# Loading the q and k rows of a graph attention layer: twelve loads of each block from GpSimd, or the late ones from SyncE inside the first pass

## The chip, the cores and the metric

One core of one Trainium2 chip runs the whole program as one launch. The metric is the device time of that core in microseconds, and lower is better. It is given as the median of three runs.

## The reference, cut to what matters

Four graph layers follow each other on 3125 nodes with 64 features and 100,000 edges. The last one is the attention layer, and the change lies around its inputs:

```python
h = jnp.maximum(_layernorm(x, axis=-1), 0.0)
q = (h[rows] @ qTrans).reshape(-1, 4, 16)
k = (h[cols] @ kTrans).reshape(-1, 4, 16)
v = (h[cols] @ vTrans).reshape(-1, 4, 16)
att = jnp.exp(jnp.clip(jnp.einsum('ehd,ehd->eh', q, k), -10.0, 10.0))
att = att / (segment_sum(att, rows)[rows] + 1e-08)
x = x + segment_sum((att[:, :, None] * v).reshape(-1, 64), rows)
```

## The kernel before, in words

The program is a sequence of three blocks, and every block ends in a barrier of all engines. `build_matrices` (line 122) scatters the edges into a dense table of edge counts and one of weights in DRAM. `propagating_layers` (line 687) runs the first three graph layers as six multiplications with these tables, and makes q, k and v for the fourth. `attention_layer` (line 1103) computes scores between all pairs of nodes and multiplies each with the edge count of the pair.

The nodes stand in 25 tiles of 128, and these in seven chunks (`CHUNKS`, line 44), six of 512 nodes and a last one of 128. At the end of `propagating_layers` TensorE projects chunk n to q and k (line 1032), and VectorE (`split`, line 895) cuts the result into three bf16 pieces; the last of the three is line 905. To reuse its piece buffer, `split(n)` waits until chunk n - 2 has been stored (line 900). GpSimd stores the pieces of chunk n in DRAM (line 1093, semaphore `rows_stored[n]`), waits until they have landed, and then issues twelve small loads (lines 1096 to 1100): six bring the k pieces and six the q pieces into the tile `held`, 16 partitions each, in the order in which the score matmuls want them. Such a load is called a placement below. A placement moves 64 KB for a chunk of 512 nodes and 16 KB for the last chunk. Then GpSimd turns to chunk n + 1:

```python
pool.wait_ge(rows_stored[n], 16)
for side, part_of in ((1, KPART), (0, QPART)):
    for i in range(NPART):
        pool.dma_start(placed[side][i * HD:(i + 1) * HD, :, cols], ...).then_inc(rows_placed[n], 16)
```

`attention_layer` goes over the q nodes in chunks (`ci`, seven passes), and in each pass over the 25 k tiles (`t`, called a step). In step t TensorE makes the scores of four heads (line 1317) from the k rows of tile t and the q rows of chunk ci, turns the edge counts of the step by four transposes (line 1324) and adds up the values of the step two before (line 1332). ScalarE takes the exponentials (lines 1192 to 1197), VectorE clips and weighs (lines 1224 to 1232), and GpSimd copies a value tile (line 1294).

SyncE loads the edge counts of each step (line 1168) into a ring of five buffers. The load of step t waits until the transposes of step t - 5 are done (line 1167). SyncE issues its loads in the order in which the program has them. In the first pass only, TensorE waits for `rows_placed[n]` ahead of the first k tile of chunk n (line 1351). Chunk 0 is waited for at the start of the block (line 1304). Passes 1 to 6 need the q rows of chunks 1 to 6, for which the same semaphores stand.

Of the kernel before, what the change touches and what calls it, by code (L numbers as in the profile page):

```python
# [16 lines left out]
P = 128  # L17
# [4 lines left out]
HD = D // HEADS  # L22
T = -(-N // P)
# [19 lines left out]
BANK = 512  # L43
CHUNKS = [(c, min(BANK, NR - c)) for c in range(0, NR, BANK)]
# [9 lines left out]
RING = 5  # L54
VW = 32
NPART = 6
QPART = [0, 0, 0, 1, 1, 2]
KPART = [0, 1, 2, 0, 1, 0]

# [9 lines left out]
def by_chunk(dram, n):  # L69

    c0, w = CHUNKS[n]
    return dram[c0 * NR:(c0 + w) * NR].rearrange("(p s c) -> p s c", p=P, s=T)


def rows_of(k):

    half = T * BANK // 2
    return [k["held"][0:NPART * HD, w * half:(w + 1) * half].bitcast(BF16).rearrange("p (h n) -> p h n", h=HEADS)
            for w in range(2)]


def gnn_layers(nc, x, src, dst, edge_weight, W_self, b_self, W_neigh, b_neigh,
               Wxz, bxz, bhz, Wxh, bxh, bhh, qTrans, kTrans, vTrans, out):
    with ExitStack() as ctx:
        def sb(name, shape, dt, c=ctx):
            return c.enter_context(nc.sbuf_tensor(name, shape, dt))

        table = nc.dram_tensor("table", [CELLS + GE, 2], F32, kind="Internal").ap()
        keys_dram = nc.dram_tensor("keys_dram", [NG, GE], F32, kind="Internal").ap()
        weights_dram = nc.dram_tensor("weights_dram", [NR * NR], F32, kind="Internal").ap()  # L90
        counts_dram = nc.dram_tensor("counts_dram", [NR * NR], F32, kind="Internal").ap()


        k = {
            "x": sb("x_nodes", [P, T, D], F32),
            "h": sb("h", [P, T, D], F32),
            "stat": sb("stat", [P, 3, T], F32),
            "acc": sb("acc", [P, T, D], F32),
            "held": sb("held", [P, T * BANK], F32),
            "ident": sb("ident", [P, P], F32),  # L100
            "deg_in": sb("deg_in", [P, T], F32),
            "deg_out": sb("deg_out", [P, T], F32),
            "w_self": sb("w_self", [D + 1, D], F32),
            "w_neigh": sb("w_neigh", [P, D], F32),
            "cheb0": sb("cheb0", [D + 1, 2 * D], F32),
            "cheb1": sb("cheb1", [P, 2 * D], F32),
            "cheb2": sb("cheb2", [P, 2 * D], F32),
            "qk": sb("qk", [D, 2 * D], F32),
            "v": sb("v", [D, D], F32),
        }  # L110
        parts_dram = nc.dram_tensor("parts_dram", [3, 2, HEADS, HD, NR], BF16, kind="Internal").ap()
        rows_placed = [ctx.enter_context(nc.semaphore(f"rows_placed{n}")) for n in range(len(CHUNKS))]
        with ExitStack() as c:
            build_matrices(nc, c, k, sb, table, keys_dram, weights_dram, counts_dram, x, src, dst, edge_weight,
                           W_self, b_self, W_neigh, b_neigh, Wxz, bxz, bhz, Wxh, bxh, bhh, qTrans, kTrans, vTrans)
        with ExitStack() as c:
            propagating_layers(nc, c, k, sb, weights_dram, counts_dram, parts_dram, rows_placed)
        with ExitStack() as c:
            attention_layer(nc, c, k, sb, counts_dram, rows_placed, out)


def build_matrices(nc, c, k, sb, table, keys_dram, weights_dram, counts_dram, x, src, dst, edge_weight,
# [564 lines left out]
                                        ALU.max, ALU.mult))  # L687


def propagating_layers(nc, c, k, sb, weights_dram, counts_dram, parts_dram, rows_placed):  # L690

    def sem(name):
        return c.enter_context(nc.semaphore(name))

    x, h, stat = k["x"], k["h"], k["stat"]
# [9 lines left out]
    resident = [k["held"][:].rearrange("p (s c) -> p s c", c=BANK), sb("resident", [P, T, BANK], F32, c)[:]]  # L705
    rest = term[:].rearrange("p t f -> p (t f)")
    parts = xs[:, 0].rearrange("p t f -> p (t f)")[:, 0:3 * BANK].bitcast(BF16).rearrange("p (b n c) -> p b n c", b=2, n=3)
    placed = rows_of(k)
    last = sb("last_chunk", [P, T, P], F32, c)
    clipped, scale = sb("deg_clipped", [P, 2, T], F32, c), sb("scale", [P, 7, T], F32, c)  # L710
    DINV, DIS, NDIS, INV, ROOT, TWICE, CHEB = range(7)
# [19 lines left out]
    h_ready, h_turned, h_copied = sem("h_ready_c"), sem("h_turned_c"), sem("h_copied_c")  # L731
    projected, values_made, values_copied = sem("projected"), sem("values_made"), sem("values_copied")
    parts_step, parts_ready = sem("parts_step"), sem("parts_ready")
    rows_stored = [sem(f"rows_stored{n}") for n in range(len(CHUNKS))]

    def tiles_of(n):
        c0, w = CHUNKS[n]
# [13 lines left out]
    with nc.Block() as block:  # L751
# [335 lines left out]
        @block.gpsimd  # L1087
        def _(pool):
            pool.wait_ge(sums_ready, NC * CHEB2 + KEPT[0] + 1)
            for n, (c0, w) in enumerate(CHUNKS):  # L1090
                cols = slice(c0, c0 + w)
                pool.wait_ge(parts_ready, n + 1)
                pool.dma_start(parts_dram[:, :, :, :, cols].rearrange("i w h d n -> (w h d) i n"), parts[:, n % 2, :, 0:w]  # L1093
                               ).then_inc(rows_stored[n], 16)
                pool.wait_ge(rows_stored[n], 16)
                for side, part_of in ((1, KPART), (0, QPART)):
                    for i in range(NPART):
                        pool.dma_start(placed[side][i * HD:(i + 1) * HD, :, cols],
                                       parts_dram[part_of[i], side, :, :, cols].rearrange("h d n -> d h n")
                                       ).then_inc(rows_placed[n], 16)  # L1100


def attention_layer(nc, c, k, sb, counts_dram, rows_placed, out):

    def sem(name):
        return c.enter_context(nc.semaphore(name))
# [5 lines left out]
    count = sb("count", [P, RING, 4, P], F32, c)  # L1112
# [11 lines left out]
    count_landed = [sem(f"count_landed{j}") for j in range(RING)]  # L1124
    counts_turned, weighted, values_added = sem("counts_turned"), sem("weighted"), sem("values_added")
# [9 lines left out]
    SC = T // 4  # L1135
# [15 lines left out]
    def over_chunks(eng, chunk):  # L1151

        with eng.Fori(0, SC) as ci:
            chunk(ci, 4)
        chunk(SC, T - 4 * SC)
# [4 lines left out]
    with nc.Block() as block:  # L1160
        @block.sync
        def _(sp):

            def chunk(ci, width):
                for t in range(T):
                    rows = by_chunk(counts_dram, t // 4)[:, bass.ds(4 * ci, width), t % 4 * P:(t % 4 + 1) * P]
                    sp.wait_ge(counts_turned, ci * T + t + 1)
                    sp.dma_start(count[:, t % RING, 0:width], rows).then_inc(count_landed[t % RING], 16)

            over_chunks(sp, chunk)  # L1170
            for f, ts in enumerate(out_parts):
                sp.wait_ge(out_ready, f + 1)
                full = slice(ts.start, min(ts.stop, T - 1))
                sp.dma_start(out[full.start * P:full.stop * P].rearrange("(t p) f -> p t f", p=P), tmp[:, full]
                             ).then_inc(out_stored, 16)
            sp.dma_start(out[(T - 1) * P:N], tmp[0:LAST, T - 1]).then_inc(out_stored, 16)
            sp.wait_ge(out_stored, 48)
# [123 lines left out]
        @block.tensor  # L1301
        def _(pe):
            pe.wait_ge(consts_set, 2)
            pe.wait_ge(rows_placed[0], 16 * 2 * NPART)
            pe.sem_inc(counts_turned, RING)
            pe.sem_inc(values_added, RING)

            def steps(ci, width, first=False):
# [27 lines left out]
                def step(t, j, n):  # L1336

                    score(t, j, ci * USES + n, ci * T + t)
                    add_values((j - 2) % RING, ci * T + t - 2)
# [4 lines left out]
                def tiles():  # L1344
                    pe.wait_ge(acc_read, ci + 1)
                    nc.tensor.matmul(acc[:, 0:W], zero_row[:, 0:P], zero_row[:, 0:W], start=True, stop=False,  # L1346
                                     skip_group_check=True)
                    if first:
                        for t in range(2, T):
                            if t * P % BANK == 0:  # L1350
                                pe.wait_ge(rows_placed[t * P // BANK], 16 * 2 * NPART)
                            step(t, t % RING, t // RING)
                        return
                    with pe.Fori(0, LOOPED // RING) as i:
                        for s in range(RING):
                            step(RING * i + 2 + s, (2 + s) % RING, i + (2 + s) // RING)
                    for t in range(2 + LOOPED, T):
                        step(t, t % RING, t // RING)
# [6 lines left out]
            def chunk(ci, width, next_width, first=False):  # L1365

                scores_of, tiles, values_of = steps(ci, width, first)
                tiles()
                for n in range(2):
                    if next_width:  # L1370
                        steps(ci + 1, next_width)[0](n)
                    values_of(T - 2 + n)
                pe.wait_ge(values_added, ci * T + T + RING)
                pe.sem_inc(acc_full, 1)
# [4 lines left out]
            with pe.Fori(1, SC - 1) as ci:  # L1379
                chunk(ci, 4, 4)  # L1380
# [32 lines left out]
```

## Time and profile before

| What | Value |
|---|---|
| median of three runs | 2637.91 us (2637.0 to 2641.92) |
| the profiled execution's own time | 2636.98 us |
| its span, first to last instruction | 2635.3 us |
| busy share of PE / DVE / ACT / POOL | 45% / 70% / 30% / 50% |
| mean granted TensorE clock | 0.982 |
| DMA, mean over the span | 204 GB/s |

PE is TensorE, PEld its weight loads, DVE is VectorE, ACT is ScalarE, POOL is GpSimd and SP is SyncE. A q behind an engine's name means its sequencer, which carries waits, drains, branches and the issue of DMAs. Line numbers are those of the kernel before. All stages come one after the other: the scatter of the edges until 1563 us, the six multiplications until about 2102 us, and the seven attention passes from 2135 us to the end.

### The profile page before, as it was taken

To read this page: it belongs to the slowest core of one execution; us is meant where nothing else is said; L and a number is where in the kernel's file an instruction comes from. 1 tells how busy PE (TensorE), PEld (TensorE's weight loads), DVE (VectorE), ACT (ScalarE), POOL (GpSimd) and SP (SyncE) were. 2 spreads that over 40 slices of the span, in tenths; PEclk is the share of its full clock that TensorE was granted. 3 is DMA by queue.
4 is the path that set the end of the run, shared out by engine and by line. 5 is a ranking of instruction groups with operands and counts; after the bars stand their busy time and mean duration, and the time that the engine had idled before them with its cause. 6 is when DMAs were issued, how large, how long until landed. Compare 5 with 4: busy or idle time off the path is not lost. (4 is left out here: it accounts for less than half of the span.)

```text
span 2635.3 us, 40047 instructions
## 1 busy us (share of the span) xinstructions
PE 1193.1 (45%) x12261; PEld 590.7 (22%) x12261; DVE 1857.5 (70%) x3958; ACT 795.0 (30%) x1929; POOL 1312.5 (50%) x1064
## 2 busy tenths in 40 slices
PE   2111111111111111111111019999999859889888
PEld 1111111111111111111111003344444412333334
DVE  9988788888888888888888510013222559999996
ACT  0000000122332233311111130000001359999996
POOL 2788888888888888888888800000000520000001
PEclk9999999999999999999999999999999879999997
DMA  7767677588988898866667599989987733333331
GB/s 231 240 192 228 195 226 202 124 211 208 225 195 223 204 223 202 218 140 130 140 137 167 116 303 424 385 342 386 424 365 277 221 94 86 86 88 88 87 88 45
DMA packets 489315, 537.88 MB, mean 204 GB/s; under 512 B 131264, under 2 KB 445117, under 8 KB 471069
## 3 DMA queue, kind: packets, MB, share of 16 engines
q1 hardware_dynamic: 123325, 283.04, 29.0%
q10 hardware_dynamic: 249904, 245.78, 28.9%
q0 software_dynamic: 116016, 8.23, 11.3%
q8 instruction: 31, 0.51, 0.1%
q14 instruction: 39, 0.32, 0.0%
HBM read 368.64 MB, written 168.31 MB: 204 GB/s over the span
## 5 line engine op out<-in xcount | busy, mean ns | idle before, releaser
L632 POOL DMA_INDIRECT table<-amount,cell x782 | 1220.1, 1560 | 294.3 <-issue 282.3
L453 DVE SCALAR_TENSOR_TENSOR equal<-key_row,keys,masks 128x1280 bf16<-128x1280 f32 (+9 forms) x790 | 692.0, 941 | 0.2 <-DVE parts L439 0.2
L585 PE MATMUL totals<-parts_g,equal 128*128 128x6 bf16 x4345 | 129.1, 167 | 1020.2 <-DVE is_tile L462 1020.0
L303 ACT ACTIVATE held<-held 128x128 f32<-128x128 f32 x600 | 179.2, 301 | 787.2 <-issue 776.4
L585 PEld LDWEIGHTS totals<-parts_g,equal 128*128 128x128 bf16 x4345 | 122.3, 104 | 1031.8 <-DVE is_tile L462 1031.4
L1063 PE MATMUL banks<-ring,xs 128*64 128x512 f32 x1200 | 290.5, 600 | 93.0 <-DMA ring<-counts_dram 91.7
L1093 POOL DMA_DIRECT2D parts_dram<-xs x7 | 5.5, 783 | 521.7 <-DVE xs L905 521.7
L1294 POOL COPY v_tile<-acc 128x64 f32 x175 | 41.5, 238 | 441.1 <-PE banks_d L1332 440.5
L445 DVE SCALAR_TENSOR_TENSOR equal_tail<-key_row,keys,masks 128x1280 bf16<-128x1280 f32 x156 | 235.2, 1545 | 18.2 <-issue 16.2
L1317 PE MATMUL banks_d<-held 96*128 (+2 forms) x700 | 192.9, 366 | 65.7 <-ACT att L1195 32.4
L1197 ACT ACTIVATE att<-att,shift 128x1024 f32<-128x1024 f32 (+1 forms) x175 | 209.5, 1197 | 0.0
L1192 ACT ACTIVATE att<-banks_d,shift 128x1024 f32<-128x1024 f32 (+1 forms) x175 | 201.5, 1151 | 19.7 <-PE banks_d L1317 19.3
L1229 DVE SCALAR_TENSOR_TENSOR att<-att,banks_d 128x1024 f32<-128x1024 f32 (+1 forms) x175 | 190.3, 1088 | 8.2 <-ACT att L1197 3.1
L1232 DVE TENSOR_TENSOR att<-att,banks_d 128x1024 f32<-128x1024 f32 (+1 forms) x175 | 188.9, 1080 | 0.0
L1195 ACT ACTIVATE att<-banks_d 128x1024 f32<-128x1024 f32 (+1 forms) x175 | 186.4, 1065 | 0.0
L1332 PE MATMUL banks_d<-att,v_tile 128*32 128x512 f32 (+1 forms) x1400 | 171.5, 565 | 0.5 <-DVE att L1232 0.5
L470 DVE TENSOR_REDUCE amount<-totals 128x20 f32<-128x60 f32 x79 | 17.4, 220 | 210.3 <-POOLq L646 160.7
L1063 PEld LDWEIGHTS banks<-ring,xs 128*64 128x64 f32 x1200 | 92.9, 137 | 261.9 <-issue 147.7
L303 ACT ACT_TABLE_LOAD x1 | 1.3, 1283 | 491.1 <-POOLq L646 491.1
L594 PE MATMUL totals<-carried_parts,equal_tail 128*128 128x6 bf16 x1560 | 54.4, 168 | 206.8 <-DVE carried_parts L490 204.3
L836 ACT COPY y_t<-banks 128x512 f32<-128x512 f32 (+1 forms) x42 | 22.7, 540 | 340.6 <-PE banks L1063 340.6
L925 DVE TENSOR_TENSOR xs<-banks,scale 128x256 f32<-128x256 f32 (+1 forms) x14 | 5.5, 396 | 164.1 <-PE banks L1009 164.1
(225 smaller groups left out, 1811.9 us busy)
## 6 DMA issues: line engine op xcount, KB each, us to landing
table<-acc ACTq DMA_DIRECT2D x100, 800.0 KB
held<-table ACTq DMA_DIRECT2D x24, 3200.0 KB
ring<-counts_dram SPq DMA_DIRECT2D x60, 1280.0 KB, 11.7
ring<-weights_dram SPq DMA_DIRECT2D x60, 1280.0 KB, 10.5
key_row<-keys_dram SPq DMA_DIRECT2D x79, 640.0 KB
weights_dram<-held ACTq DMA_DIRECT2D x24, 1600.0 KB
counts_dram<-c_tile ACTq DMA_DIRECT2D x24, 1600.0 KB
count<-counts_dram SPq DMA_DIRECT2D x150, 256.0 KB, 2.9
```

The lines of the kernel that those rows point to most:

```text
L303: ins = nc.scalar.activation(w_tile[:, b, s], cells[:, s, :, 0], ACT.Copy, accum_out=deg_parts[:, s, bass.ds(t, 1)])
L445: ins = nc.vector.scalar_tensor_tensor(equal_tail[:, b, i, :], key_row[:, b, :], keys[:, bass.ds(g * G - TAIL + i, 1)], all_mask, ALU.is_e ...
L453: ins = nc.vector.scalar_tensor_tensor(equal[b][:, OWN_AT[j]:OWN_AT[j + 1]], key_row[:, b, j * P:GE], keys[:, bass.ds(g * G + j, 1)], own_ ...
L585: nc.tensor.matmul(sums, equal[b][:, at:at + P], parts_g[:, b, j, :], start=False, stop=True, skip_group_check=True)
L632: nc.gpsimd.indirect_dma_start(out=table, out_offset=bass.IndirectOffsetOnAxis(ap=cell[:, b, j:j + 1], axis=0), in_=amount[:, b, j, :], in ...
L1063: ins = nc.tensor.matmul(banks[at:at + D, g % 2, 0:w], xs[:, prop % 2, s], rows, start=s < 2, stop=True, skip_group_check=True)
L1192: nc.scalar.activation(att[:, j, high, 0:W], scores[:, high, 0:W], ACT.Relu, bias=shift[:, 0:1]).then_inc(scores_read[1], 1)
L1195: nc.scalar.activation(att[:, j, low, 0:W], scores[:, low, 0:W], ACT.Exp).then_inc(scores_read[0], 1)
L1197: nc.scalar.activation(att[:, j, high, 0:W], att[:, j, high, 0:W], ACT.Exp, bias=shift[:, 1:2]).then_inc(expd_high, 1)
L1229: nc.vector.scalar_tensor_tensor(att[:, j, high, 0:W], att[:, j, high, 0:W], HI, times, ALU.min, ALU.mult)
L1232: nc.vector.tensor_tensor(att[:, j, low, 0:W], att[:, j, low, 0:W], times, ALU.mult).then_inc(weighted, 1)
L1317: ins = nc.tensor.matmul(scores[:, hd, 0:W], k6[:, hd, bass.ds(t * P, P)], q6[:, hd, bass.ds(ci * BANK, W)], start=True, stop=True)
```

## The change

GpSimd keeps storing all seven chunks. It places k for chunks 0 to 4 and q for chunk 0 alone. SyncE places k of chunks 5 and 6 behind its count loads 4 and 5 of the first pass (after waiting for the store of that chunk), and q of chunks 1 to 6 behind count loads 7 to 12. The semaphore `rows_placed` is split into `k_placed` and `q_placed`, and TensorE waits for `q_placed[1:]` at the end of the first pass. SyncE's first pass is written out, and its loop starts at pass 1.

```diff
+AHEAD = 5
+def place_rows(eng, k, parts_dram, side, n, placed):
+    cols = slice(CHUNKS[n][0], sum(CHUNKS[n]))
+    for i, part in enumerate((QPART, KPART)[side]):
+        eng.dma_start(rows_of(k)[side][i * HD:(i + 1) * HD, :, cols],
+                      parts_dram[part, side, :, :, cols].rearrange("h d n -> d h n")).then_inc(placed[n], 16)
...
                 pool.dma_start(parts_dram[:, :, :, :, cols].rearrange("i w h d n -> (w h d) i n"), parts[:, n % 2, :, 0:w]
                                ).then_inc(rows_stored[n], 16)
-                pool.wait_ge(rows_stored[n], 16)
-                for side, part_of in ((1, KPART), (0, QPART)):
-                    for i in range(NPART):
-                        pool.dma_start(placed[side][i * HD:(i + 1) * HD, :, cols],
-                                       parts_dram[part_of[i], side, :, :, cols].rearrange("h d n -> d h n")
-                                       ).then_inc(rows_placed[n], 16)
+                if n < AHEAD:
+                    pool.wait_ge(rows_stored[n], 16)
+                    place_rows(pool, k, parts_dram, 1, n, k_placed)
+                    if n == 0:
+                        place_rows(pool, k, parts_dram, 0, n, q_placed)
...
-            def chunk(ci, width):
+            def load(ci, width, t):
+                rows = by_chunk(counts_dram, t // 4)[:, bass.ds(4 * ci, width), t % 4 * P:(t % 4 + 1) * P]
+                sp.wait_ge(counts_turned, ci * T + t + 1)
+                sp.dma_start(count[:, t % RING, 0:width], rows).then_inc(count_landed[t % RING], 16)
+            for t in range(T):
+                load(0, 4, t)
+                n = t - RING + 1
+                if AHEAD <= n + AHEAD < len(CHUNKS):
+                    sp.wait_ge(rows_stored[n + AHEAD], 16)
+                    place_rows(sp, k, parts_dram, 1, n + AHEAD, k_placed)
+                n = t - RING - 1
+                if 1 <= n < len(CHUNKS):
+                    place_rows(sp, k, parts_dram, 0, n, q_placed)
+            with sp.Fori(1, SC) as ci:
                 for t in range(T):
...
-            over_chunks(sp, chunk)
+                    load(ci, 4, t)
+            for t in range(T):
+                load(SC, T - 4 * SC, t)
...
-            pe.wait_ge(rows_placed[0], 16 * 2 * NPART)
+            pe.wait_ge(k_placed[0], 16 * NPART)
+            pe.wait_ge(q_placed[0], 16 * NPART)
...
-                                pe.wait_ge(rows_placed[t * P // BANK], 16 * 2 * NPART)
+                                pe.wait_ge(k_placed[t * P // BANK], 16 * NPART)
...
                 tiles()
+                if first:
+                    for placed in q_placed[1:]:
+                        pe.wait_ge(placed, 16 * NPART)
```

## Rows read from the trace of the kernel before

**Rows 1.** The page, the span in 40 equal slices, TensorE.
```profile
PE   2111111111111111111111019999999859889888
```

**Rows 2.** Waits that ended between 2110 and 2240 us: total, times, longest.
```profile
PE banks_d L1317 <- ACTq L1184: 32.3, 1, 32.3
```

**Rows 3.** Line 751, the block's end: duration ns min/median/max, first and last start us.
```profile
L751 DVEq DRAIN  x1: 17/17/17, 2106.0 to 2106.0; - x1
L751 POOLq DRAIN  x1: 8400/8400/8400, 2125.9 to 2125.9; - x1
...
L751 SPq EVENT_SEMAPHORE  x1: 17/17/17, 2134.5 to 2134.5; - x1
```

**Rows 4.** Timeline of GpSimd: start us, us, instruction, and the idle time before it.
```profile
2074.40 6.09 POOL L1098 DMA_DIRECT2D held<-parts_dram  x12 [17.20 <-DMA parts_dram<-xs]
2080.48 0.77 POOL L1093 DMA_DIRECT2D parts_dram<-xs  x1
2083.73 6.09 POOL L1098 DMA_DIRECT2D held<-parts_dram  x12 [2.48 <-DMA parts_dram<-xs]
...
2118.21 0.77 POOL L1093 DMA_DIRECT2D parts_dram<-xs  x1
2120.72 6.09 POOL L1098 DMA_DIRECT2D held<-parts_dram  x12 [1.74 <-DMA parts_dram<-xs]
```

**Rows 5.** DMA issues from 2030 to 2240 us: KB each, median us to landing.
```profile
held<-parts_dram POOLq DMA_DIRECT2D x72, 64.0 KB, 2.4
parts_dram<-xs POOLq DMA_DIRECT2D x6, 384.0 KB, 3.0
held<-parts_dram POOLq DMA_DIRECT2D x12, 16.0 KB, 2.0
```

**Rows 6.** Timeline of VectorE, the last piece of chunks 3 to 6.
```profile
2083.35 0.43 DVE L905 CAST xs<-term 128x512 bf16<-128x512 f32 x1
...
2096.96 0.43 DVE L905 CAST xs<-term 128x512 bf16<-128x512 f32 x1
...
2103.81 0.43 DVE L905 CAST xs<-term 128x512 bf16<-128x512 f32 x1
...
2105.51 0.23 DVE L905 CAST xs<-term 128x128 bf16<-128x128 f32 x1
```

**Rows 7.** Windows: each engine's busy us, granted clock, DMA share, GB/s.
```profile
2040.00:2060.00 20.00, 20.00 (x106) 8.63 (x104) 8.88 (x20) 6.34 (x11) 7.98 (x14) 1.00 1.02 364
2116.00:2117.00 1.00, 0.00 (x0) 0.00 (x0) 0.00 (x0) 0.00 (x0) 1.00 (x3) 0.50 0.52 135
2128.00:2129.00 1.00, 0.00 (x0) 0.00 (x0) 0.00 (x0) 0.00 (x0) 0.00 (x0) 0.50 0.00 0
```

**Rows 8.** Line 208, the end of the block before: GpSimd's drain.
```profile
L208 POOLq DRAIN  x1: 1052/1052/1052, 1528.5 to 1528.5; - x1
```

**Rows 9.** Line 1168, the count loads until 2240 us: issue, landing, timeline.
```profile
L1168 SPq DMA_DIRECT2D count<-counts_dram x39: 346/373/400, 2135.3 to 2238.3; - x39
DMA to landing us min/median/max: 2.7/2.9/5.5
2135.26 103.42 SPq L1168 DMA_DIRECT2D count<-counts_dram  x39
```

**Rows 10.** Timeline of TensorE, the transposes of steps 0 and 13.
```profile
2138.43 1.11 PE L1324 MATMUL banks_d<-ident,count 128*128 128x128 f32 x4 [1.29 <-DMA count<-counts_dram]
...
2176.95 0.63 PE L1324 MATMUL banks_d<-ident,count 128*128 128x128 f32 x4
```

**Rows 11.** Line 248, SyncE's small loads at the start of the program.
```profile
L248 SPq DMA_DIRECT2D cheb<-in_L_gnn_Wxz_dram x5: 596/597/607, 36.5 to 39.7; - x5
...
L248 SPq DMA_DIRECT2D x_nodes<-in_x_dram x2: 1269/5684/10100, 20.7 to 22.1; - x2
...
L248 SPq DMA_DIRECT2D self_in<-in_L_gnn_W_self_dram x1: 940/940/940, 32.2 to 32.2; - x1
```

More of the change, by code:

```diff
@@ L111, in gnn_layers @@
         parts_dram = nc.dram_tensor("parts_dram", [3, 2, HEADS, HD, NR], BF16, kind="Internal").ap()
-        rows_placed = [ctx.enter_context(nc.semaphore(f"rows_placed{n}")) for n in range(len(CHUNKS))]
+        rows_stored, q_placed, k_placed = [[ctx.enter_context(nc.semaphore(f"{name}{n}")) for n in range(len(CHUNKS))]
+                                           for name in ("rows_stored", "q_placed", "k_placed")]
         with ExitStack() as c:
@@ L116, in gnn_layers @@
         with ExitStack() as c:
-            propagating_layers(nc, c, k, sb, weights_dram, counts_dram, parts_dram, rows_placed)
+            propagating_layers(nc, c, k, sb, weights_dram, counts_dram, parts_dram, rows_stored,
+                               q_placed, k_placed)
         with ExitStack() as c:
-            attention_layer(nc, c, k, sb, counts_dram, rows_placed, out)
+            attention_layer(nc, c, k, sb, counts_dram, parts_dram, rows_stored, q_placed, k_placed, out)
 def build_matrices(nc, c, k, sb, table, keys_dram, weights_dram, counts_dram, x, src, dst, edge_weight,
@@ L687, in layer_norm, with propagating_layers @@
                                         ALU.max, ALU.mult))
-def propagating_layers(nc, c, k, sb, weights_dram, counts_dram, parts_dram, rows_placed):
+def propagating_layers(nc, c, k, sb, weights_dram, counts_dram, parts_dram, rows_stored, q_placed, k_placed):
     def sem(name):
@@ L707, in propagating_layers @@
     parts = xs[:, 0].rearrange("p t f -> p (t f)")[:, 0:3 * BANK].bitcast(BF16).rearrange("p (b n c) -> p b n c", b=2, n=3)
-    placed = rows_of(k)
     last = sb("last_chunk", [P, T, P], F32, c)
@@ L733, in propagating_layers @@
     parts_step, parts_ready = sem("parts_step"), sem("parts_ready")
-    rows_stored = [sem(f"rows_stored{n}") for n in range(len(CHUNKS))]
     def tiles_of(n):
@@ L1094, in _, with attention_layer @@
                                ).then_inc(rows_stored[n], 16)
-                pool.wait_ge(rows_stored[n], 16)
-                for side, part_of in ((1, KPART), (0, QPART)):
-                    for i in range(NPART):
-                        pool.dma_start(placed[side][i * HD:(i + 1) * HD, :, cols],
-                                       parts_dram[part_of[i], side, :, :, cols].rearrange("h d n -> d h n")
-                                       ).then_inc(rows_placed[n], 16)
-def attention_layer(nc, c, k, sb, counts_dram, rows_placed, out):
+                if n < AHEAD:
[3 more added lines that the diff above has]
+                        place_rows(pool, k, parts_dram, 0, n, q_placed)
+def attention_layer(nc, c, k, sb, counts_dram, parts_dram, rows_stored, q_placed, k_placed, out):
     def sem(name):
@@ L1162, in _ @@
         def _(sp):
-            def chunk(ci, width):
+            def load(ci, width, t):
[12 more added lines that the diff above has]
+            with sp.Fori(1, SC) as ci:
                 for t in range(T):
-                    rows = by_chunk(counts_dram, t // 4)[:, bass.ds(4 * ci, width), t % 4 * P:(t % 4 + 1) * P]
-                    sp.wait_ge(counts_turned, ci * T + t + 1)
-                    sp.dma_start(count[:, t % RING, 0:width], rows).then_inc(count_landed[t % RING], 16)
-            over_chunks(sp, chunk)
+                    load(ci, 4, t)
+            for t in range(T):
+                load(SC, T - 4 * SC, t)
             for f, ts in enumerate(out_parts):
```

## The prediction, made before the changed kernel was run

> **What bounds the kernel now.** I read the page's slices first. TensorE is busy nearly throughout from slice 24 on, except for a dip around slice 32 [rows 1]. That is where the six multiplications end and the attention begins. The waits of that stretch name the dip: the first score matmul waited 32.3 us [rows 2]. The record at the block's end tells who came last. VectorE had its drain done at 2106.0. GpSimd's drain started at 2125.9 and took 8.40 us, to 2134.3, and all engines were released at 2134.5 [rows 3]. So the 28 us from 2106 to 2134 belong to GpSimd alone. Its timeline shows what it did: for each chunk a store, a wait of about 2.5 us until the store had landed, and a burst of twelve placements of 6.09 us. The last burst ran from 2120.72 to 2126.81 [rows 4]. The pieces it waited for came much earlier: the last was cast at 2105.51 + 0.23 = 2105.74 [rows 6]. GpSimd is behind by its own issuing. Behind its last issue lie another 7.5 us of drain (2126.81 to 2134.3), although the last placements take 2.0 us to land [rows 5] and nothing moved from 2128 on [rows 7].
>
> A burst costs the same 6.09 us for 64 KB and for 16 KB placements [rows 4, 5], 0.51 us each, so the issue and not the data sets it.
>
> **The change part by part.**
>
> GpSimd's chain. It loses 48 of 84 placements: 24 us of issuing at 0.51. It also loses two waits, those for stores 5 and 6. The sum cannot be 24 plus two waits, for GpSimd would then run into VectorE's pieces. I follow the chain. Chunk 0 and store 1 do not change, so GpSimd goes on at 2074.40 with six placements instead of twelve: 3.05 us, to 2077.45. A store costs 3.25 us until the burst behind it starts (2080.48 to 2083.73) [rows 4]. Chunk 2 is thus done at 2077.45 + 3.25 + 3.05 = 2083.75. Chunk 3's pieces are ready at 2083.35 + 0.43 = 2083.78 [rows 6], so it is done at 2090.1. Chunk 4's pieces are ready at 2097.39, and it is done at 2103.7. From here VectorE is the later one: chunk 5's pieces are ready at 2104.24, its store is issued by 2105.0, chunk 6's pieces are ready at 2105.74, and the last store is issued by 2105.74 + 0.77 = 2106.5. Nothing waits behind it. VectorE itself is not helped or hurt: for chunk 6 it needs store 4 landed, which comes at 2097.4 + 3.25 = 2100.7. GpSimd's last issue ends at 2106.5 instead of 2126.8, **20.3 us earlier**.
>
> The drain behind it. Of a drain behind two stores no row exists, so I bound it. Now it is 7.5 us behind the last issue [rows 3, 4]. The other end is the drain of the block before, 1.05 us [rows 8], where every DMA had landed when it began. If the drain is that short once the stores have landed (3.0 us from issue [rows 5]), it ends at 2105.74 + 3.0 + 1.05 = 2109.8; the lowest end, 1.05 us behind the last issue, is 2107.6. I take 7.5 us, as the nearest row: the same block, direct DMAs, and 6 us of it with no data moving. GpSimd's drain then ends at 2106.5 + 7.5 = 2114.0, against 2134.3. With the short drain the gain is 24.5 to 26.7 us.
>
> The loads on SyncE. It issues 48 placements, 12 for k of chunks 5 and 6 behind count loads 4 and 5, and 36 for q behind loads 7 to 12. Its waits for `rows_stored` 5 and 6 hold up count load 5 and all behind it, but the stores land by about 2109, before SyncE leaves the barrier. What matters is the count ring. SyncE starts at 2135.26 in the old time frame [rows 9]. Load 13 is the first behind all placements. It is used by the transposes of step 13, which start at 2176.95 [rows 10]. Ahead of its landing lie 14 count loads of 0.37 us plus a move, 0.41 each, so 5.7 us, then 48 placements of c us, and 2.9 us of landing [rows 9]. That fits if 48c is at most 2176.95 - 2135.26 - 5.7 - 2.9 = 33.1 us, **c at most 0.69 us**. SyncE never issued such a placement. The nearest by form is the count load, 0.37 us. The small loads of the start, by far nearer in their 64 short rows, cost 0.60 us, one of them 0.94 [rows 11]. I take 0.60 as the value, between these: no stall, with 4 us to spare. At 0.94 the stall is 48 x 0.25 = 12 us. Data does not fill the queue: the six 64 KB placements of one step are 384 KB, 2.9 us at the 135 GB/s that GpSimd's bursts reached [rows 7], and all of them together some 19 us, in 42 us.
>
> The waits on TensorE. The k rows of chunk 5 are wanted at step 20 and the q rows at the end of the pass, both behind step 13. So they cost nothing. If the cover were gone, a late q would delay pass 1 by as much as it is late.
>
> The first steps. After the gap the four transposes of step 0 took 1.11 us, those of step 13 0.63 [rows 10], since the granted clock was 0.50, the lower of its two levels (1.2 GHz), throughout the gap [rows 7]. A gap shorter by 20 us still lies in that stretch, so the start-up of the pass is moved and not changed: nothing.
>
> **Sum.** 20.3 us less, nothing given back. The profiled execution took 2636.98 us around its span of 2635.3; it would take 2616.7. The median of the runs is 0.9 us above the profiled one, so I forecast 2617.6.
>
> **The rivals.**
>
> Short drain. The 7.5 us may hang on the number of DMAs still queued (two against twelve), or only on their landing. For it speaks the 1.05 us of [rows 8], against it that in [rows 7] nothing moved in the last 6 us. Time: 2637.9 - 24.5 to 26.7 = 2611.2 to 2613.4.
>
> SyncE's issuing shows, mildly. If c is 0.7 to 1.1, TensorE waits for counts between steps 8 and 13, the stall is 0 to 20 us, at 0.94 12 us: 2629.6. For it speaks the 0.94 row, against it the 0.37 of the count loads.
>
> Slower than before. The same queue, from a definite point on: the gain of 20.3 is used up at c = 0.69 + 20.3/48 = 1.11 us, and 0.2% is lost at 1.22. Only the two loads of the nodes [rows 11], of 1.27 us and 10.1 us, were dearer; they stood behind large loads in a full queue. At 1.27 us the stall is 28 us and the time 2645.4. The place would be the transposes of line 1324 in steps 8 to 13.
>
> Nothing gained. The transfers themselves may be the bound, so that GpSimd would be held by them wherever they are issued. Against it: 16 KB and 64 KB cost the same issue, and the DMAs ran at 135 GB/s there where the same queues gave 364 in the multiplications [rows 7]. Time: 2637.9. The Trainium skill (DMA: Bandwidth & Descriptors, "Issuing engines are not separate DMA queues") speaks for this rival: all engines' DMAs run on the same 16 DMA engines, and issuing from several only saves the sequencer's issue time, which it calls usually small. By that rule the change would give little. Here the trace disagrees in the size: issuing is 0.51 us for each placement, 24 us for the 48.
>
> **How the numbers follow.** Forecast 0.52, with its own range of 2615 to 2620 (the drain and chain uncertain by 1 to 2 us); short drain, or one between the two ends, 0.28; SyncE's stall 0.13; slower 0.03; nothing gained 0.04. The range runs from 2610.5, just below the shortest drain, to 2624, which takes in stalls up to 6 us, c = 0.82. It leaves out the dearer half of the stalls and the last two cases, plus what I have not thought of. A measurement tells apart about 0.2%, 5.3 us. Faster by more than that: 0.52 + 0.28 + 0.12, so 0.92. Within it 0.05, slower 0.03.
>
> **What would show it.** In the changed trace GpSimd's last store should be issued at about 2105.7, and its drain should end at about 2114. A drain of 1 to 4 us is the short one. The wait of the first score matmul should fall from 32.3 to about 12 us. SyncE's placements should take 0.3 to 0.7 us each. TensorE's wait for counts should stay at the first step, and the first pass should last as long as now. The forecast is wrong if the drain differs by over 3 us, if TensorE waits for counts in steps 5 to 13, or if the first pass grows by over 3 us.

## The result, and the profile after

The changed kernel took 2613.82 us (median of five runs, 2613.0 to 2618.17), against 2639.74 us for the kernel before in the same comparison (2637.0 to 2641.92). The ratio is 0.9906, with a 95% interval of 0.9893 to 0.9920. The profiled execution took 2614.88 us around a span of 2613.2, which is 22.1 us less span. The medians are 25.9 us apart, and no trace accounts for the 3.8 us between the two figures: the kernel before was slower here than in its own profile (2639.74 against 2636.98 us), and the changed one faster (2613.82 against 2614.88 us).

The page's slices show the dip of [rows 1] filled. It is 7 and 9 now, where 8 and 5 stood:

```profile
PE   1111111111111111111111109999999979889888
```

The waits that ended between 2090 and 2240 us. The first line answers to [rows 2]; the second is the only wait of the transposes' matmuls for counts:

```profile
PE banks_d L1339 <- ACTq L1205: 8.5, 1, 8.5
...
PE banks_d L1346 <- DMA count<-counts_dram: 1.1, 1, 1.1
```

The block's end, now line 760 (answers to [rows 3]). VectorE is done at 2106.8, GpSimd's drain ends at 2106.8 + 4.36 = 2111.2, and all are released at 2111.3. From VectorE's end to the release it was 28.5 us and is 4.5:

```profile
L760 DVEq DRAIN  x1: 17/17/17, 2106.8 to 2106.8; - x1
L760 POOLq DRAIN  x1: 4360/4360/4360, 2106.8 to 2106.8; - x1
L760 SPq EVENT_SEMAPHORE  x1: 17/17/17, 2111.3 to 2111.3; - x1
```

The timeline of GpSimd (answers to [rows 4]). From chunk 1 on a burst has six placements and takes 3.06 to 3.42 us, and the last two stores have no burst behind them:

```profile
2074.98 3.06 POOL L87 DMA_DIRECT2D held<-parts_dram  x6 [16.64 <-DMA parts_dram<-xs]
2078.03 0.77 POOL L1102 DMA_DIRECT2D parts_dram<-xs  x1
2081.34 3.18 POOL L87 DMA_DIRECT2D held<-parts_dram  x6 [2.53 <-DMA parts_dram<-xs]
...
2105.16 0.77 POOL L1102 DMA_DIRECT2D parts_dram<-xs  x1 [0.19 <-issue]
2106.84 0.76 POOL L1102 DMA_DIRECT2D parts_dram<-xs  x1 [0.91 <-DVE xs L914]
```

The timeline of SyncE's queue in the first pass, and behind it line 87 on that queue. Bursts of six placements and count loads alternate, and load 13 leaves at 2143.06. A placement takes 0.43 us, about 0.48 with the gap behind it (2.85 / 6 = 0.475):

```profile
2111.95 2.90 SPq L1176 DMA_DIRECT2D count<-counts_dram  x5
2114.90 3.04 SPq L87 DMA_DIRECT2D held<-parts_dram  x6
...
2140.16 2.85 SPq L87 DMA_DIRECT2D held<-parts_dram  x6
2143.06 96.33 SPq L1176 DMA_DIRECT2D count<-counts_dram  x34
```
```profile
L87 SPq DMA_DIRECT2D held<-parts_dram x48: 303/426/508, 2114.9 to 2142.6; - x48
```

The first pass grew by 0.2 us at most: from the release to VectorE's copy of its result it takes 83.7 us (2111.3 to 2195.01), before 83.5 (2134.5 to 2218.04). The copy, before and after:

```profile
2218.04 0.68 DVE L1241 COPY o_t<-banks_d 128x512 f32 x1
```
```profile
2195.01 0.68 DVE L1262 COPY o_t<-banks_d 128x512 f32 x1
```

The release came 23.2 us earlier (2134.5 to 2111.3), although the block's own end slipped by 0.8 us with VectorE (2106.0 to 2106.8). Of these 23.2 us, 1.1 were given back by the end of pass 5, which the section on the hardware takes up.

### The profile page after: what moved, and what is told of

Read it like the earlier page. It is cut to its first block and busy times, and to the rows that moved or that the text cites. A ratio compares the mean times of both kernels' runs of the same rounds, so it can differ in the third digit from the quotient of the medians.

```text
span 2613.2 us, 39974 instructions
## 1 busy us (share of the span) xinstructions
PE 1194.5 (46%) x12261; PEld 590.1 (23%) x12261; DVE 1858.3 (71%) x3958; ACT 794.9 (30%) x1929; POOL 1288.5 (49%) x1016
```

## The experiments

Two things were open: what sets GpSimd's drain, and how near the count ring came to a stall. A drain is the instruction with which an engine's queue ends the block. In what follows "the tail" is the time from the end of GpSimd's last issue to the end of its drain: 7.5 us before, 3.6 us after (2107.60 to 2111.2).

### Does waiting for the landing shorten the drain?

```diff
+            for n in range(AHEAD, NC):
+                pool.wait_ge(rows_stored[n], 16)
```

> The changed kernel, but GpSimd waits at the end of the block until stores 5 and 6 have landed, and only then drains. Nothing else differs. Theory A (the drain clears up after every DMA that GpSimd issued in the block, 43 here, 91 before, so it takes longer the more there were): the wait changes nothing, since that clearing up goes on whether or not the landing is waited for; the drain still ends about 2.2 us behind the landing, 3.6 us behind the last issue. Theory B (the drain waits for DMAs that are still under way, with some microseconds of extra for those): with none under way it takes the 1.05 us of the block before, and ends 1.1 us behind the landing, 1 us earlier than now. Theory C (a fixed time behind the last issue): as A.

Line 760 and GpSimd's next instruction:

```profile
L760 POOLq DRAIN  x1: 3567/3567/3567, 2109.4 to 2109.4; - x1
```
```profile
2106.89 0.75 POOL L1102 DMA_DIRECT2D parts_dram<-xs  x1 [0.90 <-DVE xs L914]
2113.21 0.63 POOL L1307 MEMSET v_tile<- 128x640 f32 x1 [5.56 <-POOLq L760]
```

With everything landed the drain starts at 2109.4 and still takes 3.57 us. It ends at 2113.0, 1.8 us later than without the wait, and 5.3 us behind the last issue. Theory B falls, and so does theory C. Theory A as written (the clearing goes on beside the wait) falls too: the time is spent in the drain itself, and only once it has started. What the drain does in it no trace shows.

The same for the kernel before:

```diff
+            pool.wait_ge(rows_placed[NC - 1], 16 * 2 * NPART)
```

> The kernel before, but GpSimd waits for the landing of its last twelve placements ahead of its drain. Landing comes about 2 us behind the last issue, and the drain ended 7.5 us behind the last issue. Theory A (clearing up, counted by the DMAs of the block): the drain still ends about 7.5 us behind the last issue, 5.5 us or so behind the landing. Theory B (only DMAs under way cost): the drain takes 1.05 us behind the landing and the gap of TensorE shrinks by 4.5 us, from 32.3 to 28.

```profile
L751 POOLq DRAIN  x1: 7487/7487/7487, 2129.0 to 2129.0; - x1
```

The drain takes 7.49 us with nothing under way. It took 3.57 with 43 DMAs in the block and 7.49 with 91: 3.92 us for 48 DMAs, 0.082 us each, and 43 x 0.082 = 3.5 leaves nothing fixed. Both kernels were released about 2 us later with their wait (2113.1 instead of 2111.3, and 2136.6 instead of 2134.5). The one run of each took 2617.28 and 2639.97 us.

The price is GpSimd's. SyncE had issued 142 loads in this block (120 into `ring`, 22 into other tiles), and its own drain took 0.12 us, before and after:

```profile
L751 SPq DRAIN  x1: 123/123/123, 2056.3 to 2056.3; - x1
```
```profile
L760 SPq DRAIN  x1: 124/124/124, 2056.9 to 2056.9; - x1
```

### The count of DMAs: fewer, more, tiny, early

`AHEAD = 3`, so 31 DMAs on GpSimd:

> AHEAD = 3 instead of 5: GpSimd places k of chunks 0 to 2 and q of chunk 0 (24 placements and 7 stores, 31 DMAs, against 43), SyncE places k of chunks 3 to 6 in the first pass. The last two stores are the same. Theory A (0.08 us of drain for each DMA of the block, from 91 against 43): the drain ends 3.6 - 12 x 0.08 = 2.6 us behind the last issue, and the gap shrinks by 1 us. Theory B (those under way) and C (fixed part behind two stores): 3.6 us as now. SyncE has 60 placements of 0.475 us in its first pass: 28.5 us, under the budget of 33, so no wait for counts at steps 5 to 16; k of chunk 3 is wanted at step 12 and issued by step 3.

The tail is 2.8 us (2105.61 to 2108.4), as theory A has it within 0.2. SyncE issued 60 placements in the first pass. TensorE's matmuls waited for counts only at the first step, as before; its weight loads waited three more times, 0.4 to 0.6 us each between 2144 and 2151, and the pass took 82.9 us, no longer than now. The one run took 2613.29 us.

Forty-eight more DMAs, ahead of everything:

```diff
+            for i in range(48):
+                pool.dma_start(spare[0:1, i:i + 1], weights_dram[i:i + 1].rearrange("(a b) -> a b", a=1)
+                               ).then_inc(spare_landed, 16)
+            pool.wait_ge(spare_landed, 16 * 48)
             pool.wait_ge(sums_ready, NC * CHEB2 + KEPT[0] + 1)
```

> The changed kernel, in which GpSimd issues 48 more loads of a single number each at the start of the block, some 450 us ahead of its first store, and waits for all of them. 91 DMAs in the block as before the change, but 48 of them one row and long done. Theory A in its plain form (each DMA of the block costs the drain 0.082 us): the drain ends 7.5 us behind the last issue instead of 3.6, and the release moves from 2111.3 to 2115.2. Theory A' (what counts is rows, or DMAs of the last burst): 3.6 as now, or little more.

Line 761, the block's end of this kernel, and the last store:

```profile
L761 POOLq DRAIN  x1: 8273/8273/8273, 2101.2 to 2101.2; - x1
```
```profile
2101.19 0.75 POOL L1107 DMA_DIRECT2D parts_dram<-xs  x1 [0.91 <-DVE xs L915]
2109.69 0.63 POOL L1310 MEMSET v_tile<- 128x640 f32 x1 [7.76 <-POOLq L761]
```

The tail is 7.5 us (2101.94 to 2109.5): that of the kernel before, with the DMAs of the kernel after and 48 single numbers that had landed some 450 us earlier. (Its build of the matrices ended 6 us earlier, so the time of its one run, 2612.16 us, says nothing here.)

The same with 64 rows each:

```diff
+            for g in range(8):
+                for i in range(NPART):
+                    pool.dma_start(spare[i * HD:(i + 1) * HD], weights_dram[0:HD * HEADS * P // 2].rearrange(
+                        "(h d n) -> d h n", h=HEADS, d=HD)).then_inc(spare_landed, 16)
+                pool.wait_ge(spare_landed, 16 * NPART * (g + 1))
```

> As the kernel with 48 more one-number loads, but each of the 48 has 64 rows of 256 bytes, as the placements of the last chunk have, and they are waited for in eight groups of six, hundreds of us ahead of the first store. Plain theory A: 7.5 us behind the last issue. If rows count: 7.5 here and 3.6 with one-number loads. If only late DMAs count: 3.6 with both.

```profile
L761 POOLq DRAIN  x1: 8273/8273/8273, 2113.9 to 2113.9; - x1
```

The same to the nanosecond as with one row. Neither rows, nor bytes, nor lateness count; the number of DMAs that GpSimd issued in the block does. The one run took 2623.3 us. Its six multiplications lasted 7.9 us longer (from the release of the block to VectorE's end 551.4 us against 543.5), which was not followed up, so this time says nothing about the drain either.

### The two halves of the change

q alone (`AHEAD = 7`):

> AHEAD = 7: only q moves to SyncE; GpSimd places k of all chunks and q of chunk 0 (55 DMAs). Behind chunk 4's placements (done at about 2104.5) come store 5 and six placements, store 6 and six placements: 3.25 + 3.05 + 2.5 + 3.05, so the last issue ends at about 2116.5. Theory A: the drain then takes 55 x 0.082 = 4.5 us behind it, and all are released at about 2121, 10 us later than in the changed kernel and 13 us earlier than before. The drain of 3.6 us would give 2120. So of the gain of 24 us, q alone brings some 13 to 14, and k of chunks 5 and 6 the other 10.

The median was 2624.92 us, ratio 0.9951 (0.9934 to 0.9967). Its block's end:

```profile
L760 DVEq DRAIN  x1: 17/17/17, 2105.1 to 2105.1; - x1
L760 POOLq DRAIN  x1: 5417/5417/5417, 2114.4 to 2114.4; - x1
L760 SPq EVENT_SEMAPHORE  x1: 17/17/17, 2120.0 to 2120.0; - x1
```

The last issue ends at 2115.3, and the tail is 4.5 us, as expected. From VectorE's end to the release it is 14.9 us. GpSimd still waits for the landing of the last two stores:

```profile
2106.69 3.05 POOL L87 DMA_DIRECT2D held<-parts_dram  x6 [2.50 <-DMA parts_dram<-xs]
...
2112.25 3.05 POOL L87 DMA_DIRECT2D held<-parts_dram  x6 [1.75 <-DMA parts_dram<-xs]
```

k of chunks 5 and 6 alone:

```diff
+                pool.wait_ge(rows_stored[n], 16)
                 if n < AHEAD:
-                    pool.wait_ge(rows_stored[n], 16)
                     place_rows(pool, k, parts_dram, 1, n, k_placed)
-                    if n == 0:
-                        place_rows(pool, k, parts_dram, 0, n, q_placed)
+                place_rows(pool, k, parts_dram, 0, n, q_placed)
...
-                n = t - RING - 1
-                if 1 <= n < len(CHUNKS):
-                    place_rows(sp, k, parts_dram, 0, n, q_placed)
```

> The other half of the change alone: k of chunks 5 and 6 goes to SyncE, GpSimd places all of q and k of chunks 0 to 4 (79 DMAs). Its chain: chunk 4 is done some 9.35 us behind chunk 3 as before, at about 2109; then store 5 and six placements 6.3 us, store 6 and six placements 5.6 us: last issue at about 2120.7. Drain 79 x 0.082 = 6.5 us: release at about 2127.3 against 2134.5 before. So k of the two chunks alone brings some 7 us, q of six chunks alone brought 14.5 in the trace, and together they brought 23 to 24. Ratio about 0.9973.

```profile
L760 DVEq DRAIN  x1: 17/17/17, 2107.8 to 2107.8; - x1
L760 POOLq DRAIN  x1: 7377/7377/7377, 2121.2 to 2121.2; - x1
L760 SPq EVENT_SEMAPHORE  x1: 17/17/17, 2128.7 to 2128.7; - x1
```

The tail is 6.5 us (2122.05 to 2128.6), as expected. The median of ten runs was 2633.05 us, ratio 0.9981 (0.9969 to 0.9993). From VectorE's end to the release it is 20.9 us. So of the 28.5 us before, k alone takes 7.6, q alone 13.6, and both 24.0. The 2.8 us beyond the sum fit the waits for the landing of the last two stores (2.50 and 1.75 us above), which only both halves together remove, less the 0.91 us that GpSimd then waits for VectorE's last piece: 3.3 us, which leaves 0.5 unexplained.

The drains without a wait for the landing in one table, with those of the next section (us; DMAs are those that GpSimd issued in the block):

| Kernel | DMAs | last issue ends | drain ends | tail | 0.082 x DMAs |
|---|---|---|---|---|---|
| before | 91 | 2126.81 | 2134.3 | 7.5 | 7.5 |
| after with 48 tiny early DMAs | 91 | 2101.94 | 2109.5 | 7.5 | 7.5 |
| after with 48 early DMAs of 64 rows | 91 | 2114.69 | 2122.2 | 7.5 | 7.5 |
| k alone | 79 | 2122.05 | 2128.6 | 6.5 | 6.5 |
| q alone | 55 | 2115.30 | 2119.8 | 4.5 | 4.5 |
| after | 43 | 2107.60 | 2111.2 | 3.6 | 3.5 |
| last three stores on SyncE | 34 | 2090.76 | 2094.0 | 3.3 | 2.8 |
| `AHEAD = 3` | 31 | 2105.61 | 2108.4 | 2.8 | 2.5 |
| stores only | 7 | 2107.45 | 2109.3 | 1.8 | 0.6 |

From 43 DMAs on the count alone gives the tail. Below that the tail is 0.3 to 1.2 us longer than the count makes, and what adds to it stays open.

### Less on GpSimd still

The changed kernel once more, beside the next two on the same chip:

> The changed kernel itself, for comparison with the next two on the same chip: about 0.9906 of the kernel before, some 25 us less. GpSimd's drain about 3.6 us with 43 DMAs in the block.

2614.33 us (2613.33 to 2615.16), ratio 0.9906 (0.9889 to 0.9923), drain 4360 ns as before.

GpSimd stores only, and SyncE places everything:

```diff
+            for n in range(AHEAD):
+                sp.wait_ge(rows_stored[n], 16)
+                place_rows(sp, k, parts_dram, 1, n, k_placed)
+                if n == 0:
+                    place_rows(sp, k, parts_dram, 0, n, q_placed)
...
-                if n < AHEAD:
-                    pool.wait_ge(rows_stored[n], 16)
-                    place_rows(pool, k, parts_dram, 1, n, k_placed)
-                    if n == 0:
-                        place_rows(pool, k, parts_dram, 0, n, q_placed)
```

> GpSimd keeps the seven stores only; SyncE, whose ring loads are done by 2057, issues the 36 placements of the block as well as those of the first pass. GpSimd then issues 7 DMAs in the block. The drain runs so far: 7.49 us with 91 DMAs (all landed before), 3.57 with 43 (all landed before), so 0.082 us for each DMA and nothing else. Theory A (the drain clears up 0.08 us per DMA of the block, landed or not): 7 DMAs make 0.6 us; the drain ends within 1 us of the last issue and the release comes at about 2108.5 instead of 2111.3, unless the drain also waits for the landing of the last store at about 2109. Theory C (a fixed 3 to 4 us behind stores): no change, release at 2111. By A the time is 2.3 to 3 us under that of the changed kernel.

```profile
L760 POOLq DRAIN  x1: 2587/2587/2587, 2106.7 to 2106.7; - x1
L760 SPq EVENT_SEMAPHORE  x1: 17/17/17, 2109.4 to 2109.4; - x1
```

The release comes 1.9 us earlier than in the changed kernel and not 2.8. The tail is 1.8 us where the count makes 0.6. The last store, issued at 2106.70, lands 2.2 us later by the median of its kind, at 2108.9. The drain may wait for that landing; no run tests it. The median of the runs is 2614.38 us: no difference that can be measured.

The last three stores on SyncE:

```diff
+BY_POOL = 4
...
+            send(sp, range(BY_POOL, NC))
...
-            for n, (c0, w) in enumerate(CHUNKS):
...
+            send(pool, range(BY_POOL))
```

Here `send` is the old loop of stores and placements with the engine and the chunks as arguments.

> GpSimd keeps chunks 0 to 3 (34 DMAs); SyncE stores chunks 4, 5 and 6 and places k of chunk 4. GpSimd's drain then starts at about 2091 and is over by 2095, hidden behind VectorE. SyncE's drain took 0.12 us. Theory A and the account of the prediction (VectorE's last piece is the next bound): the release comes 0.3 us behind VectorE's drain, at about 2107.1, 4.2 us earlier than in the changed kernel, which makes 0.16% of the time. The rival (the first score matmul then waits for something that GpSimd's drain hid until now, such as the landing of store 5 for which SyncE waits behind count load 4): the gap shrinks less, or TensorE waits for counts at step 5.

```profile
L774 POOLq DRAIN  x1: 4141/4141/4141, 2089.9 to 2089.9; - x1
...
L774 DVEq DRAIN  x1: 17/17/17, 2106.4 to 2106.4; - x1
L774 SPq DRAIN  x1: 129/129/129, 2106.9 to 2106.9; - x1
L774 SPq EVENT_SEMAPHORE  x1: 17/17/17, 2107.2 to 2107.2; - x1
```

GpSimd's drain is over at 2094.0. The release comes at 2107.2, which is 0.8 us behind VectorE's end and 0.7 behind the end of SyncE's last issue (2106.53): of the gap this is all that is left. The median was 2613.32 us (2609.79 to 2615.45), ratio 0.9901 (0.9885 to 0.9918). The trace has the release 4.2 us earlier, and of this the medians show 1 us, which they can't tell from nothing. At the end of pass 0 the lead over the repeated changed kernel is 4.3 us (2191.12 against 2195.44), at the end of pass 5 it is 1.6 (2569.87 against 2571.44).

### How near was the count ring to a stall?

Each placement of SyncE twice, the second into a spare tile:

```diff
                     place_rows(sp, k, parts_dram, 1, n + AHEAD, k_placed)
+                    place_spare(sp, 1, n + AHEAD)
...
                     place_rows(sp, k, parts_dram, 0, n, q_placed)
+                    place_spare(sp, 0, n)
```

> The changed kernel, with each placement of SyncE issued twice, the second time into a spare tile that nobody reads. It tests the account of the count ring: 48 placements of 0.475 us take 22.8 us and leave some 8 us of slack in the changed kernel (load 13 is issued at 2143.06 and lands 3 us later, the transposes of step 13 start at 2153.9). Another 22.8 us should turn the slack into a stall of about 15 us, spread over steps 8 to 13, where TensorE's transposes wait for counts: a span about 15 us longer than that of the changed kernel. The rival (SyncE's placements are hidden whatever they are, because the queue is fed faster than it is emptied): the span as that of the changed kernel, within 2 us.

Timeline of TensorE, the transposes of steps 8 to 10, 12 and 13:

```profile
2139.25 0.63 PE L1359 MATMUL banks_d<-ident,count 128*128 128x128 f32 x4
2144.72 0.98 PE L1359 MATMUL banks_d<-ident,count 128*128 128x128 f32 x4 [2.53 <-DMA count<-counts_dram]
2151.78 1.12 PE L1359 MATMUL banks_d<-ident,count 128*128 128x128 f32 x4 [2.86 <-DMA count<-counts_dram]
...
2163.51 0.66 PE L1359 MATMUL banks_d<-ident,count 128*128 128x128 f32 x4 [1.23 <-DMA count<-counts_dram]
2169.92 1.11 PE L1359 MATMUL banks_d<-ident,count 128*128 128x128 f32 x4 [3.79 <-DMA count<-counts_dram]
```

The rival of the hidden queue falls. The transposes waited for counts in steps 9 to 13, 12.5 us in all, and the first pass took 100.9 us from the release (2111.2 to 2212.14) against 83.7: 17.2 us more where 15 were expected. SyncE's last burst ended at 2166.7, and step 13 began at 2169.92, just behind the landing. In the changed kernel the same load left at 2143.06, so it landed at about 2146.0, 7.9 us before step 13 of that kernel needed it:

```profile
2153.93 0.63 PE L1346 MATMUL banks_d<-ident,count 128*128 128x128 f32 x4
```

The span grew by more, 24.0 us, and the one run took 2638.96 us; the rest is in the later passes and is told below.

## Why the prediction was right, and where it was not

The range held the time and the direction was right. The point was 3.8 us too slow. In the profiled execution, 2616.7 us were forecast and 2614.88 measured, 1.8 less: 3.9 us less drain, but 1.1 us more because GpSimd's last issue ended later than forecast (2107.60 against 2106.5), and 1.1 us more at the end of pass 5. The other 2.0 us are not the kernel's: the forecast put the median 0.9 us above the profiled execution, and it came out 1.1 below. So in the profile two slips of 1.1 us hid over half of the error in the drain, and that is luck.

- **GpSimd's chain**: right. Burst after store 1 at 2074.98 (2074.40 forecast), last store issued at 2106.84 (2105.74). VectorE's pieces were 0.8 us later in this execution, and the chain follows them. Measured from VectorE's end, the last issue ends 0.8 us behind it, where 0.5 was forecast.
- **The drain**: the term that was mis-sized. "I take 7.5 us, as the nearest row: the same block, direct DMAs": it was 3.6. The mechanism of the gain (issues leave GpSimd, the block ends earlier) was right. The drain is no constant: it grows by 0.082 us for each DMA that GpSimd issued in the block, so moving 48 of them takes 3.9 us off it. The last issue ended 19.2 us earlier (2126.81 to 2107.60), where 20.3 were forecast, and with the shorter drain the release came 23.2 us earlier.
- **The short-drain rival**: nearer in time (2611.2 to 2613.4 us), by luck, for its reason is wrong. It held the number of DMAs still queued, or their landing, responsible. Waiting for the landing made both kernels slower, and 48 DMAs landed long ago cost as much as late ones. The count was in the rows: 91 DMAs and 7.5 us. I did not try a price per DMA because the drain of the block before, with 782 indirect DMAs, took 1.05 us [rows 8]. Why indirect ones are free of it was not tried.
- **The count ring**: right. A placement costs 0.475 us on SyncE against 0.60 taken, inside the bounds of 0.37 and 0.94. By the budget of 0.69 the slack would be 48 x (0.69 - 0.475) = 10.3 us; it was 7.9. Doubled, at 0.95 per pair, the queue stalled TensorE in steps 9 to 13. By the formula the stall is 48 x (0.95 - 0.69) = 12.5 us, and the pass grew by 17.2. Of the difference of 4.7, 4.0 us are dearer issues: SyncE's queue had no gap from 2111.78 to 2166.73, 54.95 us for 13 count loads and 96 placements, which make 50.9 at 0.41 and 0.475 us. The first five count loads took 2.98 us, and two of the sixteen bursts 4.03 and 3.75 us instead of about 2.8; why is not known.
- **The waits on TensorE**: right, none but that at the first step showed. The wait of the first score matmul fell to 8.5 us, 12 were forecast, and the difference is the drain.
- **Nothing gained, because issuing is cheap beside the transfers**: wrong here. Moved to SyncE, 48 placements still take 22.8 us of issue, on a queue that had the time. One argument against this rival misread its row: the 364 GB/s of [rows 7] were not moved by the same queues, for in that window SyncE's queue moved 6.54 MB of 7.27 and GpSimd's 0.71.

## What to carry to other kernels

Count the small DMAs that GpSimd issues ahead of a barrier twice: once for their issue (0.51 us each here) and once for GpSimd's drain at the block's end (0.082 us each here, whatever their size and age). SyncE's drain at the same barrier had no such price. Loads that are needed late belong behind the barrier on a queue with time to spare, and their budget is read from the step at which the next regular load behind them is used. Waiting for the DMAs to land before the drain did not shorten it; the wait came on top.

## What the runs showed of the hardware that was not expected

**The price of GpSimd's drain** per DMA, as above.

**The granted clock at the seams of the passes.** A window over the end of pass 5 (busy us of each engine, granted clock, DMA share, GB/s), first of the kernel before and then of the changed one:

```profile
2579.00:2593.30 14.30, 11.18 (x73) 3.32 (x72) 13.15 (x17) 11.76 (x17) 1.06 (x5) 1.00 0.08 23
```
```profile
2556.00:2571.40 15.40, 12.22 (x74) 3.37 (x72) 13.23 (x17) 11.83 (x17) 1.14 (x5) 0.88 0.09 24
```

Pass 5 took 73.9 us with a granted clock of 1.00 at its end, and 75.0 where it was 0.88. The clock fell to 0.50 near this seam in both: at about 2567.8 in the changed kernel, 3.6 us before the end of the pass, and behind its end in the kernel before (2593.3). Passes 1 to 4 take 75.3 us each at 1.00, and 75.9 to 76.5 where the clock in the 12 us around their start had a mean of 0.86, between its levels of 1.00 and 0.50. The profile of the kernel before had none of these dips, nor had those of k alone and of the two kernels with 48 early DMAs. The changed kernel had one, its repetition one in another pass, and the kernel with the late stores on SyncE three; the two of them in passes 4 and 5 are where 2.6 us of its 4.3 us went. The kernel with doubled placements had five, and passes 1 to 5 took 383.2 us in it against 376.4. No edit touches these passes, and two executions of one kernel differ in where the dip falls, so what sets it stays open. In such ways a few us won at the release can be lost again in a run.

**The lower clock level cost nothing in the first stage.** From 500 to 1000 us, kernel before and then the changed one:

```profile
500.00:1000.00 500.00, 75.27 (x2322) 68.19 (x2322) 414.78 (x1021) 137.68 (x670) 418.07 (x269) 1.00 0.84 204
```
```profile
500.00:1000.00 500.00, 75.68 (x2322) 68.35 (x2322) 415.28 (x1023) 137.94 (x672) 417.98 (x270) 0.50 0.85 204
```

TensorE, busy for 15% of the stretch, has the same busy time within 0.5% at 1.00 and at 0.50 (75.27 and 75.68 us), and the stage ends at the same time (1563.5 and 1563.3 us). Four of the five runs of the changed kernel had a mean clock of about 0.69 and one of 0.986; their spans were 2611.3 to 2616.5 us and 2611.6 us.
